# Splitting the dense weights at the start of the first mixer, slots and sends in two halves, and a shared buffer for the turned routes

## The chip, the cores and the metric

The kernel runs on one core of a Trainium2 chip. The metric is the device time of one execution in microseconds (us). The kernel before takes 1211.15 us (median of 3 runs, 1209.11 to 1211.19).

Engines are called PE (TensorE matmul; PEld is its weight load), DVE (VectorE), ACT (ScalarE), POOL (GpSimd) and SP (the engine that issues most DMAs).

## The reference, cut to what matters

Two layers over 2048 tokens of 128 features. The change touches layer 0 alone:

```python
# mixer 0: x += conv; linear attention with rotary angles (cos, sin), prefix sums over time, gate
q_phi = elu(rope(q)) + 1; k_phi = elu(rope(k)) + 1
attn = sum(q_phi * cumsum(k_phi * v)) / (sum(q_phi * cumsum(k_phi)) + 1e-06)
x = x + sigmoid(delta @ w_gate.T + b_gate) * (attn @ w_o.T)
# 4 dense experts on the layernormed x
h = layernorm(x) * ln_g + ln_b
gw = softmax(h @ w_moe_gate.T)
ffn = sum_e gw[e] * (silu(h @ w1[e].T + b1[e]) @ w2[e].T + b2[e])
x0 = x + ffn
# 16 routed experts on the layer's input x_in: top-1 by softmax(x_in @ Wg);
# each expert keeps its 160 tokens of highest probability (rank by counting larger ones)
out = gelu(x_in[idx] @ W1 + b1) @ W2 + b2, scattered back to its tokens
```

Layer 1 is a 16-head attention with relative positions and a gated mix; it takes most of the time and is not changed.

## The kernel before, in words

Each stage is a block with one hand-written program per engine, ordered by semaphores; an engine runs its program strictly in order, so a wait holds everything behind it. A block ends when all its engines have.

`mixer0` works on 4 chunks of 512 tokens (NC = 4), each with 9 units (8 value rows and the keys themselves), in "beats" u = -9 .. 45. In a beat every engine does its part of: the values and prefix sums of unit u, projections of the next chunk, and the finish of the previous chunk. DVE runs the prefix scans, the products of the angle tables, and `finish`; POOL runs half of the products and all products with the queries (`weighted`, L553); ACT evacuates PSUM. Around them, in the last beats, stands work for the next block:

* `bound_parts` (L677, DVE at u = 34): the largest absolute value of the dense first weights w1 (a 128x2048 reduce, L680) and of ln_g, ln_b. `bounds_summed` (L411, PE at u = 35) sums them over partitions; `route_top` (L687, DVE at u = 36) turns them into scales (L692, L696) and picks the routed expert of each token from the logits.
* ACT (L522, u = 37) writes `w1_high`, the scaled w1 in f16. POOL, behind all its beats, scales w1 in place (L573), writes the rest `w1_low` = w1 - w1_high (L575) and the small scales (L577, L578).
* `route_value` (L702, DVE at u = 39) takes the probability from the exponentials and splits it into three bf16 parts, with casts at L707, L709 and L711; then statistics, then at u = 41 the last chunk's attention product `attn` (L616), for which PE's output projection (L322) waits; then `route_rows` (L713) and the first tiles of the layernormed tokens (`early_tiles`).
* PE fills gaps with `spin`, matmuls whose results nobody uses.

`experts0` is the next block. PE turns the first four layernormed tiles ("HT", 0), then the one-hots and values of the routes (OT, MT; 8 groups), which ACT copies to `ohT` and `mvT` (only rows 0 to 47 are written, so DVE clears both first, L1309 and L1310), then HT 1 to 3, which DVE copies (L1324). ACT's copy of OT waits for the first tile of `h_tiles` (L1179). POOL makes the f16 parts of h per chunk (L910, L912), and clears gwT and zero (L914, L915). PE then runs 16 groups of dense experts (`first`, L1028 to L1030; `second`, L1042), and between their matmuls 64 route-counting matmuls (L1016, two PSUM banks in turn), each counted by DVE (L1274 to L1281). After the 64th, `slots` (L1288) gives each token its row; POOL then sends 16 tiles of tokens by indirect DMA (L920); SP loads them back as `xe` (L894), and PE runs the routed experts (`routed`, L1048) after dense group 10. The angle table of layer 1 is loaded at the start of the block (L888) into `keep["angle"]`, the buffer that holds cos in `mixer0`.

At the start of `mixer0` SP issues the loads x (4), w_dw, w_sq, cos, sin, b_gate, w_vrep, sel, then wq, wk, wv, bq, wo, and the names of `LATER` in order (wg, rank_order, ln_g, ln_b, w_mg, w1, b1, w2, ...).

Of the kernel before, what the change touches and what calls it, by code (L numbers as in the profile page):

```python
# [15 lines left out]
ALU = mybir.AluOpType  # L16
# [154 lines left out]
LATER = ("wg", "rank_order", "ln_g", "ln_b", "w_mg", "w1", "b1", "w2", "b2", "below", "W1", "W2", "be1", "be2")  # L171

def mixer0(nc, dram, keep, t0):
# [4 lines left out]
    with ExitStack() as ctx:  # L179
# [40 lines left out]
        s_later, s_scaled = sem("later_loaded"), sem("w1_scaled")  # L220
# [76 lines left out]
        def _(sp):  # L297
# [16 lines left out]
        def _(pe):  # L314
# [70 lines left out]
            def sums(u):  # L385
# [18 lines left out]
            def route_logits():  # L404
# [3 lines left out]
                for i in range(NT):  # L408
                    pe.matmul(L[:, i * RE:(i + 1) * RE], xnT[:, 2 + i * P:2 + (i + 1) * P], wg[:], start=True, stop=True)
# [17 lines left out]
            def beat(u, c, m, coming, going):  # L427
# [14 lines left out]
                elif u == UNITS - 1:  # L442
# [6 lines left out]
        def _(act):  # L449
# [55 lines left out]
            def beat(u, c, m, coming, going):  # L505
# [11 lines left out]
                if u == UNITS:  # L517
                    act.wait_ge(s_rd, 3)
# [10 lines left out]
        def _(pool):  # L529
# [33 lines left out]
            def beat(u, c, m, coming, going):  # L563
# [12 lines left out]
            for k, v in ((2, t0["ln_g"]), (3, t0["ln_b"])):  # L576
                pool.tensor_scalar(scales[:, k:k + 1], v[:], scales[:, 1:2], None, ALU.mult)  # L577
            pool.tensor_tensor(scales[:, 4:5], tops[:, 0:1], tops[:, 1:2], ALU.mult)  # L578

        @block.vector  # L580
        def _(dve):
# [7 lines left out]
            def projections(c, m):  # L589
                if m in (2, 4, 5):  # L590
# [54 lines left out]

            dve.memset(U[:, 0:1], 1.0).then_inc(s_unit, 1)
# [25 lines left out]
            dve.wait_ge(s_unit, 1)  # L672

# [3 lines left out]
            def bound_parts():  # L677

                dve.wait_ge(s_later, LATER_LOADS)
                dve.tensor_reduce(parts[:, 0:1], w1_all, AX_X, ALU.max, apply_absolute_value=True)  # L680
# [1850 lines left out]
```

## Time and profile before

| | |
|---|---|
| median of 3 runs | 1211.15 us |
| profiled execution | 1211.67 us, its span (first to last instruction) 1209.9 us |
| mean granted PE clock | 0.987 |
| PE busy | 1143.2 us (94%) |
| DVE / ACT / POOL busy | 825.1 (68%) / 686.0 (57%) / 839.1 us (69%) |
| `mixer0` ends, `experts0` begins | 154.6 us |

Times are microseconds from the first instruction. A row of a timeline gives start, duration, engine, line of the kernel, operation, what it writes and reads, how many instructions are merged, and in brackets the engine's idle time before it and what ended that. A clock of 1.00 is PE's full speed (2.4 GHz), 0.50 half of it (1.2 GHz).

### The profile page before, as it was taken

The page shows a single profiled execution, that of the slowest core. Times are in us where ns is not written, and L with a number is a line of the kernel's source. Part 1 is how long each engine was busy: PE and PEld are TensorE (multiplying, and loading weights), DVE is VectorE, ACT ScalarE, POOL GpSimd, SP SyncE. Part 2 cuts the span into 40 slices and gives each one's busy share as a digit, 9 for nine tenths or more (in the row PEclk, how much of TensorE's full clock was granted, in tenths as well). Part 3 has the DMA queues.
Part 4 walks back from the last instruction along what each step waited for, and adds up shares of the span by engine and source line. Part 5 has one row for each costly group of instructions (what it writes and reads, how often), then busy time and mean ns, then how long its engine had stood idle before and what let it go on. Part 6 is the DMA issues. An engine that isn't in the chain of part 4 may idle for free.

```text
span 1209.9 us, 31474 instructions
## 1 busy us (share of the span) xinstructions
PE 1143.2 (94%) x11948; PEld 755.6 (62%) x11948; DVE 825.1 (68%) x2036; ACT 686.0 (57%) x1375; POOL 839.1 (69%) x1109
## 2 busy tenths in 40 slices
PE   4899689989988999999999999999999999999997
PEld 2354456668755567666766666666676666676665
DVE  3778978813585886686687678668757867866552
ACT  2534254347424566666666656666666665665665
POOL 0778530050625788888798797888879879788895
PEclk9999899999989999999999999999999999999998
DMA  8300020022113401302132030230203204023001
GB/s 314 128 1 1 1 79 2 1 79 79 36 43 71 110 16 32 85 14 46 33 67 46 15 80 7 45 81 19 46 19 80 45 2 89 11 45 72 10 3 37
DMA packets 74891, 60.19 MB, mean 50 GB/s; under 512 B 38962, under 2 KB 69298, under 8 KB 73652
## 3 DMA queue, kind: packets, MB, share of 16 engines
q1 hardware_dynamic: 73716, 56.08, 18.7%
q0 software_dynamic: 1024, 2.09, 0.6%
q8 instruction: 95, 1.56, 0.5%
q14 instruction: 56, 0.46, 0.1%
HBM read 19.76 MB, written 4.72 MB: 20 GB/s over the span
## 4 chain that ended last, share of the span: by engine, by line
PE 67%; ACT 2%; DVE 1%; issue 1%; DVEq 0%
PE S L1962 10%; PE S L1963 10%; PE S L1964 10%; PE A L1952 9%; PE O L1976 6%; PE O L1977 5%; PE O L1974 5%; PE M L1943 3%; PE M L1920 2%; PE M L1922 2%; PE M L1921 2%; PE M L1937 1%; PE M L1930 1%; PE M L1928 1%; PE M L1929 1%
## 5 line engine op out<-in xcount | busy, mean ns | idle before, releaser
L1704 POOL TENSOR_TENSOR plow<-prob 128x512 f16<-128x512 f32 (+3 forms) x640 | 588.8, 931 | 94.4 <-ACT prob L2180 70.6
L2180 ACT ACTIVATE prob<-S,keep_sigma 128x512 f32<-128x512 f32 (+3 forms) x640 | 395.7, 625 | 265.0 <-PE S L1964 262.0
L2281 DVE CUSTOM_DVE_ANT_0 junk<-A,mask_rows,part 128x512 bf16<-128x512 f32 (+3 forms) x384 | 249.0, 649 | 98.3 <-PE A L1952 77.2
L1974 PE MATMUL O<-V,prob 128*128 128x65 f16 x2176 | 232.7, 193 | 0.2 <-POOL plow L1704 0.2
L1976 PE MATMUL O<-V,prob 128*128 128x64 f16 x2176 | 232.6, 195 | 0.0
L1977 PE MATMUL O<-V,plow 128*128 128x65 f16 x2176 | 231.7, 192 | 0.0
L1962 PE MATMUL S<-rows 97*128 97x512 f16 (+3 forms) x640 | 223.3, 349 | 3.7 <-ACT prob L2180 3.4
L1963 PE MATMUL S<-rows 96*128 96x512 f16 (+3 forms) x640 | 222.5, 348 | 0.0
L1952 PE MATMUL A<-rows 96*128 96x512 f16 (+3 forms) x640 | 221.2, 346 | 1.3 <-DVE part L2281 1.0
L1964 PE MATMUL S<-rows 96*128 96x512 f16 (+3 forms) x640 | 220.9, 345 | 0.0
L1974 PEld LDWEIGHTS O<-V,prob 128*128 128x128 bf16 x2176 | 203.0, 97 | 23.6 <-POOL plow L1704 0.3
L1976 PEld LDWEIGHTS O<-V,prob 128*128 128x128 bf16 x2176 | 202.3, 97 | 19.4
L1977 PEld LDWEIGHTS O<-V,plow 128*128 128x128 f16 x2176 | 202.0, 99 | 0.0
L2278 DVE TENSOR_REDUCE part<-A 128x1 f32<-128x512 f32 x192 | 131.9, 687 | 65.9 <-PE A L1952 63.9
L1964 PEld LDWEIGHTS S<-rows 96*128 96x128 f16 x640 | 62.7, 98 | 59.4
L1952 PEld LDWEIGHTS A<-rows 96*128 96x128 f16 x640 | 61.3, 96 | 61.5 <-DVE part L2281 2.0
L1693 POOL TENSOR_SCALAR_AFFINE_SELECT prob<-prob 128x128 f32<-128x128 f32 x256 | 79.1, 309 | 27.8 <-ACT prob L2180 26.6
L1962 PEld LDWEIGHTS S<-rows 97*128 97x128 f16 x640 | 61.9, 97 | 36.9 <-ACT prob L2180 9.3
L1963 PEld LDWEIGHTS S<-rows 96*128 96x128 f16 x640 | 63.0, 98 | 27.3
L1192 ACT ACTIVATE hid<-EH,b,scales 128x512 f32<-128x512 f32 x64 | 47.7, 775 | 54.8 <-PE EH L1030 54.3
L920 POOL DMA_INDIRECT xe_rows<-xn_tok,slot x16 | 15.8, 988 | 74.0 <-DVE slot L1296 69.5
L1042 PEld LDWEIGHTS EE<-w,hid 128*128 128x128 f32 x512 | 61.7, 192 | 2.0 <-issue 0.5
(390 smaller groups left out, 1913.5 us busy)
## 6 DMA issues: line engine op xcount, KB each, us to landing
rows<-stage_rows SPq DMA_DIRECT2D x64, 256.0 KB, 3.4
V<-stage_v SPq DMA_DIRECT2D x16, 516.0 KB, 4.6
W<-in_W SPq DMA_DIRECT2D x2, 2048.0 KB, 15.7
shifted<-turned SPq DMA_DIRECT2D x32, 128.0 KB, 2.3
rows<-stage_pos SPq DMA_DIRECT2D x64, 64.0 KB, 3.1
w<-in_w SPq DMA_DIRECT2D x2, 1024.0 KB, 9.0
xe_rows<-zero SPq DMA_DIRECT2D x1, 1280.0 KB, 5.3
ye_rows<-xe SPq DMA_DIRECT2D x5, 256.0 KB, 2.7
```

The source lines that it names most:

```text
L1693: pool.affine_select(at, at, pattern=[[1, P]], compare_op=ALU.is_ge, fill=0.0, base=0, channel_multiplier=-1).then_inc(s_cut, 1)
L1704: pool.tensor_tensor(plow[:, k % PB, 0:w], full, full.bitcast(BF16).rearrange("p (q e) -> p q e", e=2)[:, :, 1], ALU.subtract).then_inc(s_ ...
L1952: pe.matmul(out[:, 0:w], heads[h][QHI][0:RH, i * P:(i + 1) * P], heads[h][KHI][0:RH, cc * CW:cc * CW + w], start=True, stop=True).then_inc ...
L1962: pe.matmul(out[:, 0:w], kh[0:KR, k0:k1], qh[0:KR, q0:q1], start=True, stop=False, skip_group_check=True)
L1963: pe.matmul(out[:, 0:w], kl[0:RH, k0:k1], qh[0:RH, q0:q1], start=False, stop=False, skip_group_check=True)
L1964: pe.matmul(out[:, 0:w], kh[0:RH, k0:k1], ql[0:RH, q0:q1], start=False, stop=True, skip_group_check=True).then_inc(s_st, 1)
L1974: pe.matmul(both, high[:, cs, 1], vh[h][:, j, 0:HS + 1], start=(j == 0 and s == 0), stop=False, skip_group_check=True)
L1976: pe.matmul(part, high[:, cs, 1], vh[h][:, j, HS + 1:VW], start=False, stop=False, skip_group_check=True)
L1977: ins = pe.matmul(both, plow[:, n % PB, cs], vh[h][:, j, 0:HS + 1], start=False, stop=j == TPC * c + s, skip_group_check=True)
L2180: act.activation(prob[:, k % PB, 0:w], S[k % 2][:, 0:w], ACT.Exp, scale=sigma[:, 2 * p + h:2 * p + h + 1]).then_inc(s_exp, 1)
L2278: dve.tensor_reduce(out, A[g % 2][:, 0:w], AX_X, ALU.max, negate=True).then_inc(s_max, 1)
L2281: dve.tensor_tensor_reduce(junk[:, g % 2, 0:w], A[g % 2][:, 0:w], add, -1.0, before, ALU.add, ALU.min, out).then_inc(s_max, 1)
```

## The change

It has four parts.

1. The loads of w1, ln_g and ln_b move ahead of wq. `bound_parts` runs on DVE in front of the beats, `bounds_summed` on PE behind the first projection, the scales (`bound_scales`) at beat -8. ACT writes w1_high and then the scaled w1 in place at beat -8 (before: POOL); DVE writes w1_low at beat -4 (before: POOL); POOL does the small scales at beat -4.
2. `ohT` and `mvT` lie in the angle buffer. POOL clears it behind its last beat of `mixer0`, in four memsets of 128x512. DVE's two clears go, and so does ACT's wait for the first h tile. The angle load of layer 1 is issued after both halves of the slots.
3. In `experts0` POOL waits for 8 h tiles before it begins, and clears gwT and zero behind all four chunks of h parts instead of behind the first.
4. `slots` runs for tiles 0 to 7 after 32 counts, and for 8 to 15 after all 64; POOL sends each half when its slots are there.

```diff
-LATER = ("wg", "rank_order", "ln_g", "ln_b", "w_mg", "w1", "b1", "w2", "b2", "below", "W1", "W2", "be1", "be2")
+FIRST_EXPERTS = ("w1", "ln_g", "ln_b")
+LATER = ("wg", "rank_order", "w_mg", "b1", "w2", "b2", "below", "W1", "W2", "be1", "be2")
...
+            for name in FIRST_EXPERTS:
+                sp.dma_start(t0[name][:], dram[name]).then_inc(s_w1, 16)
...
-                        pe.wait_ge(s_rd, 4)
+                        pe.wait_ge(s_rd, 3)
...
-                elif u == UNITS - 1:
+                elif u == -SC:
                     bounds_summed()
...
-                elif u == UNITS + 1:
+                elif u == 1 - SC:
                     act.wait_ge(s_ln, 2)
-                    act.activation(w1_high, w1_all, ACT.Copy, scale=scales[:, 0:1]).then_inc(s_sqrt, 1)
+                    act.activation(w1_high, w1_all, ACT.Copy, scale=scales[:, 0:1])
+                    act.activation(w1_all, w1_all, ACT.Copy, scale=scales[:, 0:1]).then_inc(s_sqrt, 1)
...
+                if u == 5 - SC:
+                    pool.wait_ge(s_ln, 2)
+                    for k, v in ((2, t0["ln_g"]), (3, t0["ln_b"])):
+                        pool.tensor_scalar(scales[:, k:k + 1], v[:], scales[:, 1:2], None, ALU.mult)
+                    pool.tensor_tensor(scales[:, 4:5], tops[:, 0:1], tops[:, 1:2], ALU.mult)
             at_beats(beat)
-            pool.wait_ge(s_sqrt, 2)
-            pool.tensor_scalar(w1_all, w1_all, scales[:, 0:1], None, ALU.mult).then_inc(s_scaled, 1)
-            pool.wait_ge(s_scaled, 1)
-            pool.tensor_tensor(w1_low, w1_all, w1_high, ALU.subtract)
...
+            for k in ("Q", "K"):
+                wait_out(pool, (k, NC - 1))
+            for c in range(NC):
+                pool.memset(cos[:, span(c)], 0.0)
...
+                if m == 5 and c == 0:
+                    dve.wait_ge(s_sqrt, 2)
+                    dve.tensor_tensor(w1_low, w1_all, w1_high, ALU.subtract)
...
+            def bound_parts():
+                dve.wait_ge(s_w1, 16 * len(FIRST_EXPERTS))
+                dve.tensor_reduce(parts[:, 0:1], w1_all, AX_X, ALU.max, apply_absolute_value=True)
...
+            def bound_scales():
+                dve.wait_ge(s_rl, 1)
+                step(dve.tensor_scalar(tops[:, 0:2], BOUND, 1e-30, None, ALU.max))
+                dve.reciprocal(scales[:, 0:2], tops[:, 0:2]).then_inc(s_ln, 1)
...
             dve.wait_ge(s_unit, 1)
+            bound_parts()
...
-                if u == UNITS - 2:
-                    bound_parts()
+                if u == 1 - SC:
+                    bound_scales()
...
-        ohT, mvT = sb("ohT", [P, T], BF16), sb("mvT", [P, T], BF16)
+        ohT, mvT = (keep["angle"][:].bitcast(BF16)[:, k * T:(k + 1) * T] for k in (0, 1))
...
-            sp.dma_start(keep["angle"][:], dram["angle"]).then_inc(s_angle, 16)
             sp.dma_start(keep["mu"][:, 0, :], dram["mu"]).then_inc(s_mu, 16)
...
+            sp.wait_ge(s_slot, 2)
+            sp.dma_start(keep["angle"][:], dram["angle"]).then_inc(s_angle, 16)
             sp.wait_ge(s_sc, 16 * NT)
...
+            pool.wait_ge(s_hn, 2 * TPC)
             for c in range(NC):
...
-                if c == 0:
-                    pool.memset(gwT, 0.0)
-                    pool.memset(zero[:], 0.0).then_inc(s_zero, 1)
+            pool.memset(gwT, 0.0)
+            pool.memset(zero[:], 0.0).then_inc(s_zero, 1)
...
-            pool.wait_ge(s_slot, 1)
             for i in range(NT):
+                if i % HALF == 0:
+                    pool.wait_ge(s_slot, i // HALF + 1)
...
-            act.wait_ge(s_hn, 1)
...
-                if unit[0] == len(UNITS):
-                    slots()
+                if unit[0] == HALF * NC:
+                    slots(slice(0, HALF))
+                elif unit[0] == len(UNITS):
+                    slots(slice(HALF, NT))
...
-            dve.memset(ohT[:], 0.0)
-            dve.memset(mvT[:], 0.0)
```

The new `slots(at)` has the same six instructions as before, on half of the columns, with three completion waits instead of five. The kernel's other lines are the same.

## Rows read from the trace of the kernel before

**Rows 1.** Busy time by stage: stretch, length, PE, PEld, DVE, ACT, POOL, clock, DMA.

```profile
0.00:154.60 154.60, 123.09 (x394) 62.67 (x395) 113.01 (x214) 56.24 (x116) 90.66 (x74) 0.97 0.23 87
345.00:1209.90 864.90, 844.08 (x10376) 560.28 (x10373) 595.48 (x1443) 542.28 (x1121) 699.31 (x978) 0.99 0.21 44
```

**Rows 2.** PE's waits up to 345 us: for whom, total us, times, longest.

```profile
PE general L322 <- DVE attn L616: 9.4, 1, 9.4
...
PE EG L1056 <- DMA xe<-xe_rows: 2.6, 1, 2.6
```

**Rows 3.** Timeline of DVE, the last beats of mixer0.

```profile
124.77 2.26 DVE L680 TENSOR_REDUCE parts<-w 128x1 f32<-128x2048 f32 x1
...
133.63 0.22 DVE L610 TENSOR_SCALAR inv<-denom 128x64 f32<-128x64 f32 x1
...
135.04 4.88 DVE L707 CAST route_c<-route_b 128x16 bf16<-128x16 f32 x1
...
140.16 3.92 DVE L709 CAST route_c<-route_b 128x16 bf16<-128x16 f32 x1
...
144.23 0.17 DVE L711 CAST route_c<-route_c 128x32 f32<-128x32 bf16 x1
...
145.84 0.69 DVE L616 TENSOR_TENSOR attn<-numer,den 128x512 f32<-128x512 f32 x1
```

**Rows 4.** Timeline of POOL in the same stretch.

```profile
134.42 5.47 POOL L573 TENSOR_SCALAR w<-w,scales 128x2048 f32<-128x2048 f32 x1 [2.91 <-ACT keep_xT L522]
139.97 4.07 POOL L575 TENSOR_TENSOR keep_xT<-w,keep_xT 128x2048 f16<-128x2048 f32 x1
```

**Rows 5.** Busy time and granted clock behind three idle stretches of PE.

```profile
146.58:154.60 8.02, 7.72 (x24) 4.93 (x25) 5.44 (x24) 0.60 (x1) 0.00 (x0) 0.71 0.00 0
...
165.00:168.30 3.30, 3.30 (x11) 1.43 (x10) 2.24 (x5) 0.78 (x1) 3.14 (x5) 0.50 0.17 49
...
270.38:275.23 4.85, 4.85 (x26) 4.24 (x27) 0.00 (x0) 2.99 (x6) 0.00 (x0) 0.65 0.00 0
```

**Rows 6.** Timeline of ACT, start and end of mixer0.

```profile
30.29 0.63 ACT L461 ACTIVATE route_b<-route_c 128x512 f32<-128x512 f32 x1 [3.98 <-POOL route_c L543]
...
132.32 2.00 ACT L522 ACTIVATE keep_xT<-w,scales 128x2048 f16<-128x2048 f32 x1
```

**Rows 7.** Timeline of SP's queue: start and length of the issue.

```profile
9.07 0.65 SPq L303 DMA_DIRECT2D sel<-in_sel  x1
...
15.48 1.08 SPq L309 DMA_DIRECT2D ln_b<-in_ln_b  x1
```

**Rows 8.** DMA issues up to 45 us: KB each, us from issue to landing.

```profile
sel<-in_sel SPq DMA_DIRECT2D x1, 576.0 KB, 10.2
...
ln_b<-in_ln_b SPq DMA_DIRECT2D x1, 0.5 KB, 10.0
```

**Rows 9.** Timeline of DVE at the start of experts0.

```profile
156.83 4.92 DVE L1304 TENSOR_SCALAR s_tok<-x2T,keep_mv,keep_rstd 128x128 f32<-128x128 f32 x8
...
162.72 1.12 DVE L1304 TENSOR_SCALAR s_tok<-x2T,keep_mv,keep_rstd 128x128 f32<-128x128 f32 x4
```

**Rows 10.** Timeline of POOL, there.

```profile
158.64 1.80 POOL L914 MEMSET yeT<- 128x2048 f32 x1
```

**Rows 11.** Timeline of ACT, there.

```profile
157.03 2.71 ACT L1172 ACTIVATE ohT<-EG 48x512 bf16<-48x512 f32 x4 [0.98 <-DVE s_tok L1304]
```

**Rows 12.** Timeline of PE: its first dense matmul.

```profile
165.43 0.63 PE L1028 MATMUL EH<-w,keep_xT 128*128 128x512 f16 x1
```

**Rows 13.** Timeline of DVE, the end of the counting and beside the sends.

```profile
239.09 0.25 DVE L1291 TENSOR_REDUCE rank<-route_b 128x16 f32<-128x96 f32 x1
...
248.04 1.13 DVE L1348 SCALAR_TENSOR_TENSOR x2T<-EE,route_c,x2T 128x128 f32<-128x128 f32 x4 [5.45 <-PE EE L1042]
```

**Rows 14.** Timeline of POOL: the first of the 16 sends.

```profile
241.35 1.22 POOL L920 DMA_INDIRECT xe_rows<-xn_tok,slot  x1 [69.48 <-DVE slot L1296]
```

**Rows 15.** Timeline of SP's queue: the tokens come back.

```profile
263.07 0.84 SPq L894 DMA_DIRECT2D xe<-xe_rows  x1
```

More of the change, by code:

```diff
@@ L408, in route_logits @@
                 for i in range(NT):
-                    pe.matmul(L[:, i * RE:(i + 1) * RE], xnT[:, 2 + i * P:2 + (i + 1) * P], wg[:], start=True, stop=True)
+                    ins = pe.matmul(L[:, i * RE:(i + 1) * RE], xnT[:, 2 + i * P:2 + (i + 1) * P], wg[:], start=True, stop=True)
+                ins.then_inc(s_rl, 1)
             def bounds_summed():
@@ L644, in prefix @@
                                        ALU.add).then_inc(s_cum, 1)
+            def bound_parts():
+                dve.wait_ge(s_w1, 16 * len(FIRST_EXPERTS))
+                dve.tensor_reduce(parts[:, 0:1], w1_all, AX_X, ALU.max, apply_absolute_value=True)
+                step(dve.tensor_scalar(tops[:, 0:1], t0["ln_g"][:], X_NORM, None, ALU.mult))
+                dve.scalar_tensor_tensor(tops[:, 0:1], t0["ln_g"][:], -X_NORM, tops[:, 0:1], ALU.mult, ALU.max)
+                step(dve.scalar_tensor_tensor(tops[:, 1:2], t0["ln_b"][:], -1.0, t0["ln_b"][:], ALU.mult, ALU.max))
+                step(dve.tensor_tensor(parts[:, 1:2], tops[:, 0:1], tops[:, 1:2], ALU.add))
+                dve.tensor_scalar(parts[:, 0:2], parts[:, 0:2], H_UNIT, None, ALU.mult).then_inc(s_rd, 1)
+            def bound_scales():
+                dve.wait_ge(s_rl, 1)
+                step(dve.tensor_scalar(tops[:, 0:2], BOUND, 1e-30, None, ALU.max))
+                dve.reciprocal(scales[:, 0:2], tops[:, 0:2]).then_inc(s_ln, 1)
             dve.memset(U[:, 0:1], 1.0).then_inc(s_unit, 1)
@@ L672, in _ @@
             dve.wait_ge(s_unit, 1)
+            bound_parts()
             def bc(t, n):
                 return t.unsqueeze(2).to_broadcast([P, NT, n])
-            def bound_parts():
-                dve.wait_ge(s_later, LATER_LOADS)
-                dve.tensor_reduce(parts[:, 0:1], w1_all, AX_X, ALU.max, apply_absolute_value=True)
-                step(dve.tensor_scalar(tops[:, 0:1], t0["ln_g"][:], X_NORM, None, ALU.mult))
-                dve.scalar_tensor_tensor(tops[:, 0:1], t0["ln_g"][:], -X_NORM, tops[:, 0:1], ALU.mult, ALU.max)
-                step(dve.scalar_tensor_tensor(tops[:, 1:2], t0["ln_b"][:], -1.0, t0["ln_b"][:], ALU.mult, ALU.max))
-                step(dve.tensor_tensor(parts[:, 1:2], tops[:, 0:1], tops[:, 1:2], ALU.add))
-                dve.tensor_scalar(parts[:, 0:2], parts[:, 0:2], H_UNIT, None, ALU.mult).then_inc(s_rd, 1)
             def route_top():
                 logits = L.rearrange("p (n e) -> p n e", e=RE)
-                dve.wait_ge(s_rl, 1)
+                dve.wait_ge(s_rl, 2)
                 dve.wait_ge(s_later, LATER_LOADS)
-                dve.tensor_scalar(tops[:, 0:2], BOUND, 1e-30, None, ALU.max).then_inc(s_rd, 1)
                 step(dve.tensor_reduce(rmax, logits, AX_X, ALU.max))
@@ L695, in route_top @@
                 dve.tensor_tensor(cand, logits, bc(rmax, RE), ALU.is_ge).then_inc(s_rd, 1)
-                dve.reciprocal(scales[:, 0:2], tops[:, 0:2]).then_inc(s_ln, 1)
-                dve.wait_ge(s_rd, 4)
+                dve.wait_ge(s_rd, 3)
                 step(dve.tensor_tensor(cand, cand, rank_order[:].unsqueeze(1).to_broadcast([P, NT, RE]), ALU.mult))
@@ L883, in experts0 @@
         ROUTED_AT = 10
+        HALF = NT // 2
         block = ctx.enter_context(nc.Block())
@@ L1284, in count_rows, with slots @@
                 unit[0] += 1
-                if unit[0] == len(UNITS):
-                    slots()
-            def slots():
-                dve.wait_ge(s_rc, len(UNITS))
-                step(dve.tensor_reduce(rank[:], counts[:], AX_X, ALU.add))
-                step(dve.tensor_scalar(over[:], rank[:], float(CAP) - 0.5, float(2 * SLOT_ROWS), ALU.is_ge, ALU.mult))
-                step(dve.tensor_scalar(slotf[:], cmax[:], -float(CAP), float(CAP * RE), ALU.mult, ALU.add))
-                step(dve.tensor_tensor(slotf[:], slotf[:], rank[:], ALU.add))
-                step(dve.tensor_tensor(slotf[:], slotf[:], over[:], ALU.add))
-                dve.tensor_copy(slot[:], slotf[:]).then_inc(s_slot, 1)
+                if unit[0] == HALF * NC:
+                    slots(slice(0, HALF))
+                elif unit[0] == len(UNITS):
+                    slots(slice(HALF, NT))
+            def slots(at):
+                dve.wait_ge(s_rc, at.stop * NC)
+                dve.tensor_reduce(rank[:, at], counts[:, at, :], AX_X, ALU.add)
+                step(dve.tensor_scalar(slotf[:, at], cmax[:, at], -float(CAP), float(CAP * RE), ALU.mult, ALU.add))
+                dve.tensor_tensor(slotf[:, at], slotf[:, at], rank[:, at], ALU.add)
+                step(dve.tensor_scalar(over[:, at], rank[:, at], float(CAP) - 0.5, float(2 * SLOT_ROWS), ALU.is_ge, ALU.mult))
+                step(dve.tensor_tensor(slotf[:, at], slotf[:, at], over[:, at], ALU.add))
+                dve.tensor_copy(slot[:, at], slotf[:, at]).then_inc(s_slot, 1)
             def route_counts(k):
```

7 lines of the change are left out of this document (2 added, 5 removed).

## The prediction, made before the changed kernel ran

> **What bounds the kernel now.** I read busy time by stage first. PE is the bound of layer 1 (844 of 865 us busy) and much less so of `mixer0` (123 of 155) [rows 1], so a cut in layer 0 must be looked for in its waits and its chains of engines; layer 1 only moves earlier with it. PE's waits up to 345 us name two that the change can reach: 9.4 us for `attn` at the end of `mixer0`, and 2.6 us for the routed tokens `xe` [rows 2]. Why `attn` is late stands in DVE's timeline: two casts of 128x16 take 4.88 and 3.92 us where a later cast of 128x32 takes 0.17, and they end at 139.92 and 144.08 [rows 3]. POOL's two 128x2048 instructions of the w1 split end at 139.89 and 144.04 [rows 4]. So each cast stands still until a POOL instruction ends. Last, the clock: behind each idle stretch of PE it is at its lower level for some time (mean 0.71, 0.50, 0.65 in three stretches) [rows 5], so a removed stall gives back more than its own length.
>
 The trace agrees to 0.04 us at both casts.
>
> I make the sum against the profiled execution, 1211.67 us with a span of 1209.9; the median of the runs is 0.5 us lower.
>
> **Part 1, the end of `mixer0`: 10.9 us less.**
> - The casts: 4.88 + 3.92 - 2 x 0.17 = 8.5 us of standing still before `attn` [rows 3]. POOL now has no w1 work there. Late next are PE's own spins and the inverse of the denominators, which are already done.
> - The start of that chain, the inverse at 133.63 [rows 3]: DVE loses the reduce of 2.26 us [rows 3] and five small ones ahead of its last scan, about 3.6 us together. But the product in front of that scan waits for PE's projection, so the scan comes 1.0 us earlier, not 3.6; PE loses its small matmul. ACT loses the 2.00 us of w1_high, under which it had no late work [rows 6]. I take 1.0; bounds 0 and 1.9 (the wait for the logits' read-out, if it were all).
> - The clock: of the 8.02 us from 146.58 on, the mean of 0.71 says that 4.7 us ran at the lower level [rows 5]. At the upper one that work takes 2.3 us less. Of this DVE's route rows, which run between `attn` and the gated product, let some 1.4 through. Bounds 0.5 and 2.3.
> - Added: POOL clears the angle buffer in four memsets. A memset of 128x2048 took 1.80 us [rows 10], so 1.8 to 2.2. They start behind the last query product, 1 us earlier than before (at 130.5), and end by 132.6; the first cast comes near 134. Cover 1.5 us; without it the casts wait up to 2 us (a rival below). Cos has been read long before.
>
> 8.5 + 1.0 + 1.4 = 10.9; between 9.0 and 12.7.
>
> **Part 1, the start: 0.7 us more.** Everything hangs on when w1, ln_g and ln_b have landed (call it L). sel is issued at 9.07 and lands 10.2 us later, at 19.3 [rows 7, 8]; w1 is next in the queue with 1024 KB. 576 to 1024 KB at the rate of some 410 GB/s seen in this stretch are 2.5 us: 21.8. The last of the small loads, ln_b, landed at 15.48 + 10.0 = 25.5 in its old place, and such loads followed each other at 0.2 to 1.3 us [rows 7, 8]. I take L = 22.4, bounds 21.9 and 24. From there: reduce 2.26 [rows 3], five small DVE instructions 1.4, PE and its handover 0.4, scales 0.5, ACT twice 2.00 [rows 6]: ACT is free at L + 8.6 = 31.0. Its relu for the first keys started at 30.29 [rows 6], and from there ACT's table loads set the pace up to the first prefix. So the loss is L - 21.7 = 0.7; bounds 0 and 2.3.
> DVE's w1_low (two-operand, 2048 columns, some 2.3 us, the reduce being the nearest row at 2.26) comes in its idle time before the first keys' exponential; if POOL's query sum holds it up, it is 1.3 us later and still ahead of the point where DVE waits for ACT again. POOL's three small instructions stand in its idle time. PE's small matmul delays the key projection only if L is beyond 22.1. All other loads land 2.5 us later, and are needed 80 us later.
>
> **Parts 2 and 3, the start of `experts0`: 2.8 us less.** DVE loses its two clears of the route rows. Its 8 h tiles took 4.92 us, ending 1.3 us after POOL's clear of gwT ended (158.64 + 1.80) [rows 9, 10]; four free ones take 1.12 [rows 9], so the eight 2.24, and now POOL waits for them. ACT's copies lose their wait for the first h tile: 0.98 us [rows 11]. In a walk from wait to wait, HT 1 now finds DVE free and is bound by ACT's eight copies; HT 3, and with it PE's first dense matmul at 165.43 [rows 12], comes 2.1 us earlier. That matmul and those behind it ran at clock 0.50 for 3.3 us [rows 5]; with the idle stretch shorter that may go (1.5 us); I count half. Bounds 1.0 and 3.7. gwT and zero are cleared some 9 us later; first use of gwT is 12 us behind that, and the fill of the rows that waits for zero lands some 30 us before the first send. The later angle load (1024 KB) lands beside the second sends, 13 us ahead of the next transfer in SP's queue; it holds up only its issue, 0.3 us.
>
> **Part 4, slots in the counting: 0.9 us more.** The slots are six small instructions in a row, the first 0.25 us [rows 13]. Now some 1.2 us of them stand after the 32nd count, where DVE has no gap and PE's next counting matmul waits for a bank. DVE's small waits for PE later in the group give a part back. Bounds 0 and 1.3.
>
> **Part 4, the sends: 3.4 us less.** 16 sends run from 241.35 to 263.07, where `xe` is issued [rows 14, 15]: 1.36 us each. It lands 7.3 us later, at 270.38, after PE has waited 2.6 us [rows 2]. With half of the sends done before, `xe` lands 8 x 1.28 = 10 us earlier; PE's dense group 10 then ends last and the 2.6 us go. The stretch behind it is bound by ACT's copies of PE's turned tiles, 4.85 us at clock 0.65 [rows 5]; at full clock 4.1. 2.6 + 0.75 = 3.4; bounds 2.6 and 4. What holds the first sends: POOL has only them in its queue, and 24 us to the second half.
>
> **Sum.** 0.7 - 10.9 - 2.8 + 0.9 - 3.4 = -15.5: 1196.2 for the profiled execution, 1195.7 for the median.
>
> **Rivals.**
> - *The clears take the lock in place of the split.* If the four memsets still run when the casts come, the casts wait for the last. For it: a single h tile took the rest of a POOL memset [rows 9, 10]. Against: 1.5 us of cover. Price 2 us: 1197.7.
> - *The first sends slow the counting.* They are the first indirect DMAs beside DVE's busy stretch. If each locked DVE for its 0.98 us, 7.8 us: 1203.5. Against: DVE's additions beside the sends take 1.13 us for four [rows 13], as elsewhere. 
> - *The early split starves the start: slower.* If ln_b's semaphore came only when the big expert weights have landed (L = 41.5, all loads done), ACT and the first keys would be late by L - 21.7 = 19.8 instead of 0.7 us: 1195.7 + 19.1 = 1214.8. It decides where L - 21.7 is 15.5 + 0.7, from L = 37.9 on. For it: small transfers of 4 bytes a partition behind long queues took 10 us. Against: landings follow the order of issue [rows 7, 8].
>
> **How the numbers follow.** Forecast 0.75, clears 0.08, sends 0.07, casts 0.05, slower start 0.03, and 0.02 for none of them. The forecast's own bounds add up to 1190 to 1202, all ends at once; half of that width to each side is likelier, so 1191.5 to 1201.5 would be its range. I widen the upper end to 1202.5, for the rivals on that side. A measurement tells 0.2% (2.4 us) from no change: faster 0.95, same 0.01, slower 0.04.
>
> **What would show it.** Right: casts at L707 and L709 of about 0.2 us; PE's wait for `attn` near 1 us and clock 1.00 behind it; `experts0` beginning near 144.4; first dense matmul near 153; no wait of PE for `xe`, with xe issued some 8 us before PE needs it; the first relu near 31.0. Wrong: a DVE start of the w1 reduce beyond 24; casts over 1 us; PE waiting for counts by more than 2 us over before; a first dense matmul still at the lower clock.

## The result, and the profile after

The kernel after takes 1199.08 us (median of 4 runs, 1197.80 to 1199.45), the kernel before in the same sitting 1210.88 (4 runs): ratio 0.9904, 95% interval 0.9886 to 0.9921. That is 11.8 us less; 15.2 were forecast. The profiled execution took 1197.80 us, its span is 1196.1. It is the fastest of the four, so span against span the gain is 13.8 us, and the balance below is made in these.

Stages first, columns as in [rows 1]: layer 0 up to the start of `experts0`, and layer 1.

```profile
0.00:147.52 147.52, 123.84 (x395) 62.32 (x395) 108.47 (x216) 58.10 (x117) 84.97 (x76) 0.98 0.24 91
332.50:1196.10 863.60, 841.31 (x10374) 558.69 (x10372) 597.28 (x1442) 543.01 (x1121) 699.33 (x978) 1.00 0.21 44
```

`mixer0` has lost 7.1 us of length and none of PE's work: what went was waiting. PE's waits up to 345 us, as in [rows 2]:

```profile
PE values L387 <- DVE kv L641: 3.8, 2, 2.9
...
PE denom L419 <- DVE parts L665: 2.2, 1, 2.2
...
PE general L326 <- DVE attn L627: 0.9, 1, 0.9
```

The 9.4 us for `attn` are 0.9, the line for `xe` is gone, and a line that the kernel before didn't have has come: 2.2 us for the parts of the bounds, at the start. The tail of `mixer0` on DVE, which answers [rows 3]:

```profile
136.66 0.23 DVE L621 TENSOR_SCALAR inv<-denom 128x64 f32<-128x64 f32 x1 [0.80 <-PE denom L404]
...
138.08 0.17 DVE L723 CAST route_c<-route_b 128x16 bf16<-128x16 f32 x1
138.29 0.17 DVE L724 TENSOR_TENSOR route_b<-route_b,route_c 128x16 f32<-128x16 f32 x1
138.49 0.17 DVE L725 CAST route_c<-route_b 128x16 bf16<-128x16 f32 x1
...
140.41 0.69 DVE L627 TENSOR_TENSOR attn<-numer,den 128x512 f32<-128x512 f32 x1
```

and on POOL, where the clears stand in place of [rows 4]:

```profile
134.61 1.92 POOL L586 MEMSET keep_angle<- 128x512 f32 x4
```

Both casts take 0.17 us. The clears end at 136.53, 1.55 us ahead of the first. The windows for the clock (the last two answer to the second and third of [rows 5]; the first two are at the start, where before had 1.00):

```profile
28.93:32.93 4.00, 4.00 (x7) 1.39 (x6) 1.85 (x3) 3.63 (x3) 1.83 (x4) 0.60 1.03 420
39.00:42.70 3.70, 3.70 (x6) 1.54 (x5) 2.75 (x4) 1.51 (x3) 0.20 (x1) 0.55 0.25 94
...
156.20:159.50 3.30, 2.91 (x14) 1.06 (x13) 2.96 (x9) 2.28 (x3) 3.14 (x5) 1.00 0.02 5
258.38:263.00 4.62, 3.92 (x30) 3.13 (x28) 1.13 (x4) 3.39 (x6) 0.00 (x0) 1.00 0.00 0
```

The balance, by the time at which each milestone is reached (us; read from the timelines):

| milestone | before | after | gap | added by the stage | forecast |
|---|---|---|---|---|---|
| fourth scan of `mixer0` | 44.51 | 48.62 | +4.11 | +4.1 | +0.7 |
| block of `experts0` starts | 154.60 | 147.52 | -7.08 | -11.2 | -10.9 |
| first dense count | 167.38 | 157.70 | -9.68 | -2.6 | -2.8 |
| second slots cast | 240.21 | 230.69 | -9.52 | +0.2 | +0.9 |
| first expert matmul | 274.41 | 261.56 | -12.85 | -3.3 | -3.4 |
| layer 1 starts | 349.57 | 336.72 | -12.85 | 0.0 | 0 |
| end | 1209.9 | 1196.1 | -13.8 | -0.95 | 0 |

Every stage of layer 0 but the first is within 0.8 us of its term. The last row is chance: the code of layer 1 is the same, and from its first turning matmul to the end it took 859.0 to 860.4 us in the fourteen traces of this case (860.4 before, 859.3 after). The start costs six times what was forecast. Its rows, on DVE:

```profile
23.43 2.29 DVE L660 TENSOR_REDUCE parts<-w 128x1 f32<-128x2048 f32 x1 [3.86 <-DMA ln_b<-in_ln_b]
...
26.26 1.00 DVE L665 TENSOR_SCALAR parts<-parts 128x2 f32<-128x2 f32 x1
...
33.59 2.28 DVE L607 TENSOR_TENSOR keep_xT<-w,keep_xT 128x2048 f16<-128x2048 f32 x1
35.78 1.75 DVE L613 SCALAR_TENSOR_TENSOR phi<-route_c,route_b 128x512 f32<-128x512 f32 x1
```

on PE:

```profile
27.32 0.38 PE L419 MATMUL denom<-parts,keep_ones 128*128 128x2 f32 x2 [2.19 <-DVE parts L665]
...
38.48 3.31 PE L387 MATMUL values<-x1T,w_vrep 128*128 128x512 f32 x4 [2.86 <-DVE kv L641]
```

on ACT (the relu of [rows 6], 2.11 us later):

```profile
32.40 0.63 ACT L466 ACTIVATE route_b<-route_c 128x512 f32<-128x512 f32 x1 [0.37 <-POOL route_c L549]
```

and on POOL:

```profile
26.21 1.03 POOL L543 TENSOR_TENSOR delta<-x1T 128x512 f32<-128x512 f32 x1 [23.09 <-ACT x1T L461]
...
33.81 3.17 POOL L549 TENSOR_TENSOR route_c<-route_c,route_a 128x512 f32<-128x512 f32 x1 [0.75 <-DVE route_a L604]
```

The reduce starts when ln_b lands, and the loads say why that is late. DMA issues, KB each and us to landing:

```profile
w<-in_w SPq DMA_DIRECT2D x1, 1024.0 KB, 11.6
ln_g<-in_ln_g SPq DMA_DIRECT2D x1, 0.5 KB, 12.2
ln_b<-in_ln_b SPq DMA_DIRECT2D x1, 0.5 KB, 13.3
```

and the windows there (last two columns: DMA share and GB/s):

```profile
20.00:21.00 1.00, 1.00 (x2) 0.47 (x2) 0.00 (x0) 0.00 (x0) 0.00 (x0) 1.00 0.32 99
21.00:22.00 1.00, 1.00 (x2) 0.34 (x1) 0.00 (x0) 0.00 (x0) 0.00 (x0) 1.00 0.43 152
```

Issued at 9.04, 9.56 and 10.05, they landed at 20.6, 21.8 and 23.4 by this view. Only the last of the three times is sure. The loads share one semaphore, to which each adds 16, and the view takes every sixteenth count for a landing, whichever load it came from. The last packet of w1 (they are the ones of 8192 bytes) ended at 21.1. Where w1 has a semaphore of its own (e1, f1, e7 and f3 below) it landed 0.3 us behind its last packet, so here it was there near 21.4 (an estimate), and DVE could have had it some 2.0 us earlier than it did. Between 20 and 22 us, where before moved 400 to 410 GB/s, the queues' share was 0.32 and 0.43 while the small loads, 4 bytes a partition, passed.

What followed, in order:

- The last small instruction of the bounds (L665) took 1.00 us where it takes 0.17 in f1 (L666 there), and ended at 27.26, with POOL's product of 26.21 to 27.24. PE waited 2.19 us for it and ran at the lower clock level behind the wait.
- w1_low held POOL's sum (3.17 us for 1.27), and the sum held `phi` (1.75 for 0.69). That is the Trainium skill's rule in "SBUF — State Buffer", "Who interferes with whom", that a VectorE instruction with two inputs in SBUF contends with a GpSimd one that reads SBUF; the two rows agree. These two locks did not move the first scan: it stood 8.16 us behind the relu, 8.16 before, and 8.14 in e7, where w1_low is not there.
- PE waited 2.86 us for `kv` and fell to the lower level again. From the first scan to the fourth it took 8.06 us, where before took 6.06.

So the 4.1 us are 2.1 by which the relu came later, and 2.0 behind the second fall of the clock.

### The profile page after: what moved, and what is told of

Its sections match the earlier page's. It is cut to its first block, busy times and chain, and to the rows that moved or that the text cites. A ratio compares the mean times of both kernels' runs of the same rounds, so it can differ in the third digit from the quotient of the medians.

```text
span 1196.1 us, 31475 instructions
## 1 busy us (share of the span) xinstructions
PE 1138.2 (95%) x11940; PEld 751.9 (63%) x11948; DVE 819.7 (69%) x2041; ACT 688.4 (58%) x1376; POOL 832.8 (70%) x1111
## 4 chain that ended last, share of the span: by engine, by line
PE 68%; ACT 2%; DVE 1%; issue 1%; DVEq 0%
PE S L1980 10%; PE S L1981 10%; PE S L1982 10%; PE A L1970 9%; PE O L1994 6%; PE O L1995 5%; PE O L1992 5%; PE M L1961 3%; PE M L1938 2%; PE M L1940 2%; PE M L1939 2%; PE M L1955 1%; PE M L1948 1%; PE M L1946 1%; PE M L1947 1%
## 5 line engine op out<-in xcount | busy, mean ns | idle before, releaser
L1061 PE MATMUL EE<-w,hid 128*128 128x128 f32 x512 | 62.7, 275 | 0.2
```

Of the source, the lines that this page charges most:

```text
L1061: ins = pe.matmul(E[n % 2][:, i * P:(i + 1) * P], hid[:, n % 2, hb, i * P:(i + 1) * P], w2[:, e * HB + hb, :], start=hb == 0, stop=hb == H ...
```

## The experiments

Each is compared with runs of the kernel before on the same chip in the same sitting. In the second sitting (a0, e4, e5 and e7) every kernel, the one before included, ran about 20 us longer, so only ratios are carried from it.

### Is the start's loss the wait for the small loads?

e1_split_wait, on the kernel after:

```
-  sp.dma_start(t0[name][:], dram[name]).then_inc(s_w1, 16)
+  sp.dma_start(t0[name][:], dram[name]).then_inc(s_w1 if name == "w1" else s_re, 16)
...
-  dve.wait_ge(s_w1, 16 * len(FIRST_EXPERTS))
+  dve.wait_ge(s_w1, 16)
   dve.tensor_reduce(parts[:, 0:1], w1_all, ...)
+  dve.wait_ge(s_re, 32)
...
-  dve.wait_ge(s_re, 1)
+  dve.wait_ge(s_re, 33)
```

> The changed kernel, but DVE's w1 reduce waits for w1's load alone, and the wait for ln_g and ln_b stands behind the reduce (PE's and ACT's programs unchanged). Theory A (the two small loads are late, PE waits 2.2 us for the sum of the bounds, and the clock falls behind that and behind the next wait): the reduce starts near 20.7 instead of 23.4, PE's wait for it falls from 2.2 us to under 0.5, no lower clock between 28 and 33, the first relu near 30.2 instead of 32.4, the first scan near 38.6 instead of 40.6 and the fourth near 45 instead of 48.6; time 3 to 4 us less than the changed kernel, about 1195.5. Theory B (the loss at the start is the added work itself: ACT's two copies, DVE's w1_low and the lock it takes): first relu earlier by 2 us but the fourth scan by at most 1; time within 1 us of 1199.

Measured: 1196.09 us (1194.98 to 1196.90, 5 runs; before 1211.45 in 15), ratio 0.9873 [0.9855, 0.9890]. The reduce started at 22.51, when w1 had landed (22.4), and not at the 20.7 of the expectation, which took the view's 20.6 for w1's landing. The small loads had both landed at 24.4. The queues' share was 0.39 and 0.66 from 20 to 22 us here too, ahead of w1's end. The fourth scan came at 45.13. A second time, on another chip:

> The kernel after with the first reduction waiting for w1 alone, a second time, beside the kernel before. Theory (the start's loss is the wait for the small loads and what follows from it, the bounds that TensorE waits for and its fallen clock): ratio to before 0.987 to 0.989, reduction at 22.3 to 23.0 us, last product of the mixer at 136 to 138, casts 0.17 us each. Rival (the first reading was a lucky draw and the kernel is like the kernel after): ratio 0.990 to 0.992. If engines stand still for about 3 us several times between 200 and 330 us again, that belongs to the chip and adds 15 to 20 us to all the kernels, the kernel before too.

Measured: 1195.63 (1194.86 to 1197.69, 5 runs; before 1209.99 in 11), ratio 0.9882 [0.9861, 0.9902]; reduce 22.53, first relu 30.20 (before 30.29), fourth scan 44.41 (before 44.51). PE's waits in its first 60 us:

```profile
PE values L387 <- DVE kv L641: 3.3, 2, 2.8
...
PE denom L419 <- DVE parts L666: 0.5, 1, 0.5
```

The start's loss is gone in this execution, and 0.6 us of it are left in e1's. Four executions let the reduce wait for w1 alone (e1, f1, e7, f3): reduce at 22.2 to 22.5, fourth scan at 44.4 to 45.1. The seven that keep the kernel after's order and wait have them at 23.0 to 25.0 and 45.7 to 49.3, so the two groups don't meet. By the ratios the two kernels with this edit alone (e1, f1) are 2.7 to 3.8 us faster than the kernel after; the intervals still touch.

The other way about, the small loads issued ahead of w1, with one wait for all three:

```
-FIRST_EXPERTS = ("w1", "ln_g", "ln_b")
+FIRST_EXPERTS = ("ln_g", "ln_b", "w1")
```

> The kernel after with the loads of ln_g and ln_b issued ahead of w1 instead of behind it; the reduction still waits for all three. Theory (the start pays for small loads only because they stand last, in a stretch where the queues are nearly idle): the reduction starts when w1 has landed, 22.0 to 23.0 us, TensorE waits under 1.5 us for the bounds, fourth scan at 44.4 to 46 us, last product of the mixer at 136 to 138.5, 1195.5 to 1197 us, ratio 0.987 to 0.989, the same as the split wait. Rival (each small load costs its time in the queues wherever it stands, and w1 only lands that much later): the reduction at 23.5 to 24.5, TensorE waits 2.2 us for the bounds, fourth scan at 47 to 49 us, 1198 to 1200 us.

Measured: 1199.53 (1197.03 to 1200.82, 6 runs; before 1211.52 in 11), ratio 0.9897 [0.9874, 0.9920]; fourth scan 49.70. In the trace the rival holds; the median is in its range as well, but its interval covers the split wait and the kernel after alike. Its windows, and the start of its reduce:

```profile
17.00:18.00 1.00, 1.00 (x7) 0.96 (x5) 0.00 (x0) 0.45 (x1) 0.00 (x0) 1.00 0.56 204
18.00:19.00 1.00, 0.37 (x2) 0.00 (x0) 0.00 (x0) 0.74 (x2) 0.00 (x0) 1.00 0.60 225
```

```profile
24.62 2.29 DVE L660 TENSOR_REDUCE parts<-w 128x1 f32<-128x2048 f32 x1 [3.84 <-DMA w<-in_w]
```

The idle stretch of the queues moved with the small loads, from 20 to 22 us to 17 to 19 us, and w1 landed at 24.5, for 22.1 to 22.4 where it goes first and has its own semaphore. So in this one execution the two loads cost their time ahead of w1 as well; what took it away was not waiting for them.

### What does the clock add?

e2_spins gives PE work to do while it waits for the bounds and for `kv`:

```
+  if u == -2:
+      spin(("Y", 1), 2)
...
+  if u == -SC:
+      spin(("K", 0), 2)
```

> The changed kernel, but PE runs two unused f32 512-column matmuls ahead of its wait for the bounds, and two more at beat -2 ahead of its wait for the value rows; loads, ACT and DVE are unchanged. Theory A (the clock's fall is half of the start's 4.1 us): granted clock 1.00 from 20 to 45, the reduce still at 23.4, first scan 0 to 0.6 us earlier than 40.56, fourth scan 2 us earlier than 48.62; time 2 to 3 us less than 1199. Theory B (the added work is the loss): clock 1.00 too, but scans at the same times or 1 us later; time 1199 to 1200.

Measured: 1197.98 (1195.73 to 1199.40, 4 runs), ratio 0.9882 [0.9859, 0.9905]. The clock stayed at 1.00 through the start and, though the reduce began 1.1 us later than in the kernel after (24.51), the fourth scan came 1.7 us earlier (46.95). The nearest execution without the spins is e3's, where the last of the three loads landed 4.93 us behind sel as here (4.65 in the kernel after): PE's wait 2.65 us against 0.94 here, the relu 9.34 us behind the reduce against 8.23, the fourth scan at 47.96. The median is 1.1 us under the kernel after's, within the intervals. Its profiled execution lost clock elsewhere, at the end of the scans:

```profile
127.00:130.00 3.00, 3.00 (x11) 2.08 (x11) 0.32 (x1) 0.20 (x1) 0.69 (x1) 0.55 0.00 0
130.00:133.00 3.00, 3.00 (x5) 1.34 (x4) 0.94 (x2) 0.00 (x0) 1.26 (x1) 0.50 0.00 0
```

All traces of kernels whose reduce comes at the start, in the order of PE's wait for the bounds (the clock is the mean from 4 to 10 us behind the start of the reduce):

| execution | reduce starts | PE's wait | clock | reduce to relu |
|---|---|---|---|---|
| e1, e5 | 22.51, 23.04 | none | 1.00, 1.00 | 8.39, 8.43 |
| f1, e7 | 22.53, 22.25 | 0.5 | 1.00 | 7.67, 7.99 |
| e4, f2, a0 | 24.13, 24.74, 24.98 | 0.9 | 1.00 | 7.68, 7.68, 7.67 |
| e2, f3 | 24.51, 22.19 | 0.9 | 1.00 | 8.23, 7.98 |
| after | 23.43 | 2.2 | 0.72 | 8.97 |
| f4 | 24.62 | 2.4 | 0.72 | 9.67 |
| e3 | 24.40 | 2.7 | 0.78 | 9.34 |

The three long waits, and they alone, are followed by the lower level, and there the relu comes 0.5 to 2.0 us later behind the reduce. That is not the clock alone. A part is the lock seen above: POOL's first product held one of DVE's small instructions by 0.8 us in the kernel after and in f4, by 0.3 in e3 and by 0.55 in e2. The rest shows on ACT, which was done with its two copies and still waited for the keys: 0.37 us in the kernel after, 1.07 in f4, 1.08 in e3, and nothing in e2, f1 and f2. So the first fall cost 0.4 to 1.1 us.

How long PE waits for the bounds goes with how far the last of the three loads lands behind sel, with which PE's work ahead of the wait begins: 4.6 to 4.9 us in the kernel after, f4 and e3, but 4.2, 4.1, 3.8 and 2.8 in e4, a0, f2 and e5.

The second fall is not regular. Behind a wait for `kv` of 2.85 or 2.86 us the clock fell in the kernel after, in e4 and in a0, and behind one of 2.74 in f4; behind the same 2.85 it did not in f1 and f2, nor behind the 1.1 to 1.9 us of the other executions. With a fall it took 7.05 to 8.50 us from the first scan to the fourth, without one 6.06 or 6.07 in every execution, the kernel before's included. So the second fall cost 1.0 to 2.4 us, and the kernel after's own start varies: its fourth scan came at 45.7 to 49.3 us over the six executions with its loads, wait and order and no spins (after, e3, e4, e5, f2, a0), the median 47.5, 3.0 us behind before. The profiled 4.1 is on the dear side.

### Do the clears have cover?

e3_clears_late lets POOL clear the angle buffer only behind the last reciprocal of the denominators, just ahead of the casts:

```
+  pool.wait_ge(s_rec, NC)
   for c in range(NC):
```

> The changed kernel, but POOL begins its four clears of the angle buffer only when DVE has inverted the last denominators, so that they run beside DVE's casts. Theory A (a cast in SBUF waits for any POOL instruction in progress, one that only writes as well): a cast of 0.17 us becomes 0.3 to 0.7 us, or both together take up to 1.9 us; attn 0.5 to 1.6 us later; time 0.5 to 1.6 us over 1199. Rival (the casts were held by what POOL's two w1 instructions read, or by themselves; a clear holds nobody): casts 0.17 us each, time as the changed kernel.

Measured: 1200.80 (1198.75 to 1201.87, 4 runs), ratio 0.9915 [0.9894, 0.9935]. DVE:

```profile
137.40 0.56 DVE L724 CAST route_c<-route_b 128x16 bf16<-128x16 f32 x1
...
138.21 0.25 DVE L726 CAST route_c<-route_b 128x16 bf16<-128x16 f32 x1
...
138.59 0.37 DVE L728 CAST route_c<-route_c 128x32 f32<-128x32 bf16 x1
```

and POOL:

```profile
136.95 1.97 POOL L587 MEMSET keep_angle<- 128x512 f32 x4 [2.95 <-DVE inv L623]
```

Right on top of the clears, the casts wait 0.67 us together (137.40 to the end of the third at 138.96, where 0.89 would do), not the 2 us of my rival: the first ends at 137.97, behind the second clear (137.94), the second at 138.46 behind the third (138.43), the last at 138.95 behind the fourth (138.92). So a clear, which only writes, holds a cast, but the casts got through between clears of 0.5 us, where the split's one instruction of 2048 columns took 5.47 us [rows 4]. Lost cover would have cost a third of what I priced. From the last scan to `attn` it took 9.01 us against 8.35 in the kernel after, which agrees; the median time, 1.7 us over, has an interval that overlaps the kernel after's.

### What is the w1 split at the start worth?

e6_no_part1 is the kernel before with parts 2 to 4 alone (split, reduce and loads in their old places).

> The kernel before with parts 2 to 4 of the change, without part 1: the split of w1 stands at the end of the first mixer and on POOL again. Theory A (part 1 saves 11.2 us at the end and costs 4.1 at the start): casts of 4 to 5 us again, start as before (first scan near 38.5), time 7 us over the changed kernel, about 1206. Rival (the casts' stall is gone through something else of the change, such as the order of the last beats): casts short, time under 1199.

Measured: 1205.45 (1204.01 to 1210.30, 10 runs), ratio 0.9960 [0.9944, 0.9976]. Its casts:

```profile
135.51 4.88 DVE L711 CAST route_c<-route_b 128x16 bf16<-128x16 f32 x1
...
140.64 3.91 DVE L713 CAST route_c<-route_b 128x16 bf16<-128x16 f32 x1
```

Its ten executions spread over 6 us. By the medians parts 2 to 4 are worth 6.0 us by themselves (1211.45 - 1205.45; in the balance -2.6 + 0.2 - 3.3 = -5.7), and part 1, its loss at the start taken off, the other 5.8 of the 11.8 (in the balance -11.2 + 4.1 = -7.1).

### A second sitting: the kernel after, and parts 2 to 4 taken apart

> The changed kernel again, word for word, on the chip of the three runs below. Theory A (the start's loss hangs on when ln_b lands, 4.7 to 5.0 us behind sel, and on whether PE's clock falls once or twice behind the two waits): the w1 reduce between 23.3 and 24.6, fourth scan between 47.5 and 49, executions spread over 2 us or more; median 1199 to 1200. Rival (the first profile was an unusual one): reduce near 22.4 and fourth scan below 46.

a0 is the kernel after itself: 1221.06 (1218.91 to 1223.53, 6 runs; before 1230.41 in 18), ratio 0.9918 [0.9890, 0.9947]. e5_pool_first takes POOL's clears back to the front of its queue:

```
-  pool.wait_ge(s_hn, 2 * TPC)
...
+  if c == 0:
+      pool.memset(gwT, 0.0)
+      pool.memset(zero[:], 0.0).then_inc(s_zero, 1)
```

> The changed kernel, but POOL starts at once in experts0 and clears gwT and zero behind the first chunk, as before; DVE's two clears stay away and ACT doesn't wait. Theory A (most of the 2.6 us of this stage comes from keeping POOL out of DVE's h tiles): one h tile waits for POOL's clear again (over 2 us), first dense matmul 1 to 2.5 us later than 8.7 us behind the block's start; 1 to 3 us more, about 1201. Rival (it comes from ACT's missing wait and the missing clears alone, the tiles being covered by ACT's eight copies): h tiles slow, but the first dense matmul moves by less than 0.5 us, and so does the time.

Measured: 1221.32 (7 runs), ratio 0.9923 [0.9899, 0.9947]. DVE and POOL:

```profile
144.68 5.30 DVE L1324 TENSOR_SCALAR s_tok<-x2T,keep_mv,keep_rstd 128x128 f32<-128x128 f32 x8
148.12 1.86 DVE L1332 RECIPROCAL keep_rstd<-std0b 128x4 f32<-128x4 f32 x1
```

```profile
147.95 1.81 POOL L932 MEMSET yeT<- 128x2048 f32 x1
```

The lock is back. One of the eight tiles took 3.20 us for 0.34, from 146.78 to 149.98, across three instructions of POOL that followed without a gap (its subtraction and both clears, the last ending at 149.90); in the kernel before one took 3.20 as well, across the same three. And it costs nothing: the first dense matmul stands 8.69 us behind the start of the block, 8.68 in the kernel after, 10.83 before. In the kernel after the tiles (the row of [rows 9])

```profile
147.60 2.13 DVE L1324 TENSOR_SCALAR s_tok<-x2T,keep_mv,keep_rstd 128x128 f32<-128x128 f32 x8
```

end 2.2 us behind the start of the block, in e5 5.4, before 7.2. So what paid was part 2: DVE without its two clears of 0.91 us ahead of the first tile, and ACT without its wait for that tile. No run parts these two.

e4_slots_whole undoes part 4: slots in one piece behind the counting, and all 16 sends and the angle load behind them.

```
-  if i % HALF == 0:
-      pool.wait_ge(s_slot, i // HALF + 1)
+  if i == 0:
+      pool.wait_ge(s_slot, 1)
...
-  if unit[0] == HALF * NC:
-      slots(slice(0, HALF))
-  elif unit[0] == len(UNITS):
-      slots(slice(HALF, NT))
+  if unit[0] == len(UNITS):
+      slots(slice(0, NT))
```

> The changed kernel with slots and sends in one piece behind the 64th count, as before. Theory A (the sends hold xe back): PE waits for xe again, 2 to 3 us, then runs at the lower clock over the turned tiles; first expert matmul behind xe 3.7 us later, less 0.5 us that the half slots cost in the counting: 3.2 us more, about 1202.5. Rival (the halves only moved the wait): within 1 us of the changed kernel.

Measured: 1221.20 (8 runs), ratio 0.9914 [0.9890, 0.9938], the same as a0, which tells nothing: in this sitting PE stood still in the sends' stretch (4.1 us up to 243.3), as the traces beside it do (last section), and the tokens landed before it needed them. So again, on another chip:

> The kernel after with slots and sending in one piece as in the kernel before, a second time. Theory (halving the sends is worth what the transposes of the received tokens waited before, 2.6 us, less the half-way slots that counting pays, 0.5): 1.5 to 3 us slower than the kernel after on the same chip, ratio to before 0.991 to 0.994; TensorE waits 2 to 3.5 us for the received tokens at about 265 us, at a lower granted clock behind the wait. Rival (the wait is covered by work that TensorE has left, or its time is given back): ratio 0.9895 to 0.991, wait under 1 us.

Measured: 1202.39 (1199.11 to 1203.78, 6 runs), ratio 0.9937 [0.9918, 0.9955], against 0.9904 for the kernel after. Its wait, and PE's timeline:

```profile
PE EG L1075 <- DMA xe<-xe_rows: 2.2, 1, 2.2
```

```profile
257.83 4.24 PE L1075 MATMUL EG<-keep_ident,xe 128*128 128x128 f32 x20 [2.22 <-DMA xe<-xe_rows]
261.91 1.25 PE L1084 MATMUL ER<-xeT,W 128*128 128x160 f32 x8
```

The wait is back, and so is the lower clock (0.77 from 260 to 264). From the slots to the first expert matmul it takes 34.1 us where the kernel after takes 30.9, so 3.2 us (3.4 forecast), and the counting is 0.9 us shorter without slots in its middle (72.1 for 73.0; 0.9 forecast). Net 2.3 in the profile; the ratios differ by 0.0033, 4 us, with intervals of 2 us either way.

### Is VectorE's low part of w1 in the way?

e7_low_at_end is e1 with that subtraction moved to the last scans:

```
-  if m == 5 and c == 0:
-      dve.wait_ge(s_sqrt, 2)
-      dve.tensor_tensor(w1_low, w1_all, w1_high, ALU.subtract)
...
+  if u == UNITS - 2:
+      dve.wait_ge(s_sqrt, 2)
+      dve.tensor_tensor(w1_low, w1_all, w1_high, ALU.subtract)
```

> The kernel whose reduce waits for w1 alone (1196.1 us), with DVE's w1_low moved from beat -4 to beat 34, where DVE idles 2.5 us for PE's projection. Theory A (w1_low costs something at the start through the ports that it shares with POOL's query sum): the first value product 0.5 to 1.5 us earlier relative to the reduce, the end of the mixer later by 0.2 to 1; net 0 to 1 us less, about 1195.7. Rival (its place at the start is free, since ACT sets the pace there): scans at the same distance from the first relu, and the end later by 0.2 to 2.3; 1196 to 1198.

Measured: 1218.59 (1215.43 to 1219.16, 6 runs), ratio 0.9893 [0.9864, 0.9921], with e1's 0.9873 in the other sitting. The trace is the rival's: the first scan stood 8.14 us behind the relu against 8.16 in e1, and the last `attn` 91.80 us behind the fourth scan against 91.81. Beside f1 it was run again:

> The reduction waiting for w1 alone, and VectorE's own low part of the first layer's weights put near the end of the scans, a second time. Theory (at the start the low part takes VectorE about 1 us that the chain of scans waits for; at the end it is covered by TensorE): 0.5 to 1 us faster than the split wait alone, first scan at 38.2 to 38.6 us against 39.1. Rival (the first scan comes earlier but the low part at the end is waited for): first scan earlier, last product not, ratios alike within 0.1%.

Measured: 1197.10 (1194.84 to 1199.25, 6 runs), ratio 0.9892 [0.9871, 0.9912] against f1's 0.9882. My theory fell: the first scan came at 38.31 us against 38.35. In f1 the second key's phi waits for ACT anyway (its end moves nothing). At the other end the subtraction takes 2.58 us and is covered too: `attn` stood 93.50 us behind the fourth scan against 93.48. So the low part costs nothing in either place. One thing speaks for the late one: PE's wait for `kv` at the start was 1.89 us in e7 and f3 against 2.85 in f1, and the clock fell behind none of 1.9 us or less. e1 had 1.68 with the low part at the start, so this stays open.

## Why the prediction was right, and where it was not

- **Casts, 8.5 us.** Shown: 0.17 us each without POOL's w1 work, 4.88 and 3.91 with it (e6).
- **Chain and clock of the tail, 1.0 + 1.4.** The last two scans stood 4.34 us apart against 5.30, so 1.0; from `attn` to the block 7.11 us against 8.76, so 1.65. The size was right, but the tail has a chance of its own: in six executions of changed kernels (after, e1, e3, e5, e7, f2) the clock stayed at 1.00 there and the gap was 4.33 or 4.34 us, in six others (e2, e4, a0, f1, f3, f4) it fell to means of 0.56 to 0.77 between these two scans and the gap was 5.10 to 6.94. The two executions with the split at the end (before, e6) had 1.00; two are too few to say that the change brings this on.
- **Clears under cover.** 1.55 us, 1.5 forecast; the rival's price was too high (e3).
- **Start of `experts0`, 2.8.** 2.6 measured, but the working gave the credit for the tiles to both edits. e5 gives it all to part 2: a DVE stall was removed by part 3 that nothing waited for. The clock behind the first dense matmul was 1.00 and gave 0.45 (1.95 us from it to the first count, then 1.50), and in the next stage 0.7 more: the counting took 72.8 us before and 72.1 in f2, which has the slots in one piece too, and before ran at the lower level up to 168.3 [rows 5]. Together 1.15, for 0.75 forecast.
- **Slots, 0.9, and sends, 3.4.** 0.9 and 3.2 by f2 against the kernel after. The balance's +0.2 is this 0.9 less the 0.7 of the clock. The sends did not slow the counts: a count of 512 columns took 0.75 us at most in the kernel after, beside the first eight sends as elsewhere. Why is not shown by this; the Trainium skill's "SBUF — State Buffer", "Who interferes with whom", which the prediction cites for it, names instructions with at most one input in SBUF and outside the two-port modes, and does not mention PSUM.
- **The start, 0.7: the step that failed.** "I take L = 22.4" put 0.6 us for both small loads on top of w1's 21.8, from the 0.2 to 1.3 us by which such loads followed each other at the end of the load queue. Where w1's landing can be told from theirs (e1, f1, e7, f3), w1 came at 22.1 to 22.4 and they were there 2.0 to 2.6 us later. Over the seven executions with this wait and order the reduce started at 23.0 to 25.0, in five of them beyond my upper bound of 24. From L on, the sum was right by luck: relu at L + 8.6 is 32.03, measured 32.40, but in f1, f2, e4 and a0, with no lock and no fall of the clock, it is L + 7.7. The lock of 0.8 us on L665, which the working did not have, made the two agree. "PE's small matmul delays the key projection only if L is beyond 22.1" was written and then not priced: L was beyond it, PE waited 2.2 us, and the two falls of the clock followed. The second, 2.0 us of the 4.1, had no term at all, since the working stopped at the relu. The bounds 0 to 2.3 did not hold the 4.1, nor the 3.0 of the median execution.

In the profile the sum was 1.7 us off (13.8 for 15.5), less than the start alone, because chance gave 1.0 in layer 1 and the counting cost 0.7 less than its term. The median gain fell 3.4 us short of the forecast; that the start's excess in the profile is 3.4 too is a coincidence. The split wait has the lowest ratios measured, 0.9873 and 0.9882 in two sittings; its intervals still touch the kernel after's.

## What to carry to other kernels

Bring work forward only with the loads that it needs first: wait for the large operand by itself, and for the small ones where they are read. Loads that share a semaphore have no landing time of their own in the trace, so give one that you want to time a semaphore of its own. A stall found in a trace is worth what the next stage's slack leaves of it, so ask for each of several edits which of them ends the wait last. When a stall of PE of some microseconds is made or removed, look at the granted clock behind it too, at both ends of the change.

## What the runs showed of the hardware that was not expected

- Two loads of 0.5 KB (4 bytes on each of 128 partitions) went with some 2 us in which the queues' share was 0.3 to 0.7, behind a large load (after, e1) as well as ahead of it (f4). It is not regular: in two of the twelve executions with these loads at the start the share stayed at 0.89 and more there (a0) and at 0.96 and more (e5). In e5 they landed 2.8 us behind sel, in a0 still 4.1.
- POOL's instructions in a row can hold one of DVE across several of them: a tile of 0.34 us took 3.20 across three (before, e5). In e3 casts got through between the four clears. What makes the difference stays open.
- In the second sitting all four traces have three or four waits of PE of 1.7 to 6.2 us between 200 and 330 us; the other traces have none over 1.6 there, but for those for `xe`. In each trace, three to six times, PE, DVE and ACT stood still together for 0.5 to 3.6 us. In a0 PE's last matmul before a halt started at 247.13, and DVE and ACT, which waited for its results, went on only at 250.5, while POOL's sends kept their pace (246.71, 247.99). DVE, ACT and PE of a0, the idle time of the first two put down to "remote" by the profile:

```profile
250.48 1.12 DVE L1366 SCALAR_TENSOR_TENSOR x2T<-EE,route_c,x2T 128x128 f32<-128x128 f32 x4 [9.68 <-remote]
250.54 1.45 ACT L1210 ACTIVATE hid<-EH,b,scales 128x512 f32<-128x512 f32 x2 [7.08 <-remote]
...
251.38 0.39 PE L1047 MATMUL EH<-w,keep_xT 128*128 128x512 f16 x1 [3.86 <-ACT hid L1210]
```

  One of the other sittings was on the very same chip. What causes the halts stays open; the kernel before took 19 us more in that sitting too, so they are not the change's.
